# A vision block on one core: the mixer's two norms moved to ACT, the third Newton step to GpSimd

## What is computed

```python
# token mixer, per image: h is (256, 256)
y = sigmoid(q) * (ew @ (exp(k) * v)) / (ew @ exp(k))
h = y @ out_w + out_b + flatten(x)
h = (h - mean(h)) * rsqrt(var(h) + 1e-05) * ln_g + ln_b        # first norm

# a class token is put in front, then attention with mixed heads
xn = (h - mean(h)) / sqrt(var(h) + 1e-05)                      # second norm
q, k, v = split(xn @ w_qkv)                                    # 16 heads of 64
attn = softmax(q @ k.T / 8)
attn = einsum('bhij,hg->bgij', attn, reattn_w)                 # heads are mixed
attn = (attn - mean_g(attn)) * rsqrt(var_g(attn) + 1e-03)      # norm over the 16 heads
h = h + (attn * gamma + beta) @ v @ w_out + b_out

# feed-forward with quantized activations and ternary weights
h = h + quant(silu(quant(norm(h)) @ w_gate.T) * (... @ w_up.T)) @ w_down.T
```

## Time and profile before

| what | value |
|---|---|
| median of 3 runs | 852.46 us (850.26 to 853.55) |
| the profiled execution | 854.99 us, its span 853.2 us |
| busy: PE, DVE, ACT, POOL | 81%, 66%, 51%, 25% of the span |
| mean granted PE clock | 0.933 of full |

### The profile page before, as it was taken

The page is one execution under the profiler, slowest core; times in us unless marked ns, Lnnn a source line. Parts: engine busy times, 40 slices in busy tenths (PEclk is TensorE's granted clock), DMA queues, the critical chain, the costliest instruction groups (busy, mean ns, idle before and its releaser), DMA issues.

```text
span 853.2 us, 18885 instructions
## 1 busy us (share of the span) xinstructions
PE 691.6 (81%) x7618; PEld 483.0 (57%) x7634; DVE 566.3 (66%) x1215; ACT 436.1 (51%) x1231; POOL 212.2 (25%) x399
## 2 busy tenths in 40 slices
PE   0859758997889978998899888987899789757654
PEld 0546545766567646765576656764676567535421
DVE  0596647566876788568956786678767885559333
ACT  0103706583566657473748354755666574738311
POOL 0307224102430154014411233024301540033000
PEclk9959967999799999999999979999999999979977
DMA  8400560047102531145005610362025301450000
GB/s 317 159 1 6 176 240 2 1 147 250 40 3 77 187 141 33 45 157 203 33 15 173 216 32 2 112 232 93 2 79 198 129 8 50 152 202 10 1 12 1
DMA packets 42395, 83.98 MB, mean 98 GB/s; under 512 B 3003, under 2 KB 6596, under 8 KB 41668
## 3 DMA queue, kind: packets, MB, share of 16 engines
q1 hardware_dynamic: 41268, 79.29, 27.0%
q10 hardware_dynamic: 1040, 3.49, 1.0%
HBM read 46.98 MB, written 35.79 MB: 97 GB/s over the span
## 4 chain that ended last, share of the span: by engine, by line
PE 39%; DVE 21%; DMA 21%; ACT 10%; issue 6%; POOL 2%; SPq 1%; POOLq 0%; ACTq 0%; DVEq 0%
DMA pg<-turned 12%; DMA turned<-pst 8%; PE big L546 7%; PE small L546 7%; PE big L563 6%; PE small L707 4%; DVE var L1246 4%; DVE an L1290 3%; ACT pst L941 3%; PE small L692 2%; PE big L640 2%; PE small L662 2%; ACT ot L1029 2%; ACT sqb L961 2%; DMA tok_b<-in_tok_b 2%
## 5 line engine op out<-in xcount | busy, mean ns | idle before, releaser
L941 ACT ACTIVATE pst<-big,nb 128x256 f32<-128x256 f32 x256 | 117.9, 474 | 32.0 <-DVE nb L1214 32.0
L1211 DVE TENSOR_REDUCE mx<-big 128x4 f32<-128x1024 f32 x64 | 78.3, 1223 | 52.3 <-PE big L563 51.6
L640 PEld LDWEIGHTS big<-pst,pg 64*64 64x64 f32 x4096 | 72.8, 149 | 52.5 <-DVE an L1290 28.3
L640 PE MATMUL big<-pst,pg 64*64 64x64 f32 x4096 | 80.6, 236 | 21.9 <-DVE an L1290 12.2
L961 ACT ACTIVATE sqb<-big 128x1024 f32<-128x1024 f32 x64 | 65.2, 1020 | 35.7 <-PE big L640 33.8
L1246 DVE TENSOR_REDUCE var<-sqb 128x64 f32<-128x1024 f32 x64 | 77.4, 1211 | 7.5 <-ACT sqb L961 7.5
L1290 DVE TENSOR_TENSOR an<-big,rstd 128x1024 f32<-128x1024 f32 x64 | 78.4, 1224 | 2.2
L662 PE MATMUL small<-w_qkv,xnv 128*128 128x512 f32 x128 | 69.9, 672 | 8.5 <-DVE h L1383 5.7
L563 PE MATMUL big<-qk_t 64*128 64x256 f32 x512 | 72.6, 402 | 3.8 <-ACT qk_t L924 3.7
L692 PE MATMUL small<-an,v 128*64 128x130 f32 (+1 forms) x768 | 56.6, 289 | 21.2 <-ACT ot L1029 20.6
L546 PE MATMUL small<-xnt,w_qkv 128*128 128x256 f32 x256 | 63.8, 392 | 0.0
(11 more groups left out here) (201 smaller groups left out, 1262.8 us busy)
## 6 DMA issues: line engine op xcount, KB each, us to landing
turned<-pst SPq DMA_DIRECT2D x128, 257.0 KB
pg<-turned SPq DMA_DIRECT2D x16, 2056.0 KB, 11.0
w_qkv<-in_w_qkv SPq DMA_DIRECT2D x1, 3072.0 KB
xt<-in_x_t SPq DMA_DIRECT2D x8, 256.0 KB, 2.9
xr<-in_x_tok SPq DMA_DIRECT2D x8, 256.0 KB, 2.7
out<-h SPq DMA_DIRECT2D x16, 128.0 KB
an<-in_gate_t ACTq DMA_DIRECT2D x1, 1024.0 KB, 8.6
an<-in_up_t ACTq DMA_DIRECT2D x1, 1024.0 KB, 10.9
```

What stands on the lines that cost most here:

```text
L640: last = mm(mix_place(n)[half[0]:half[1], k_hi * 512 + i * 64:k_hi * 512 + (i + 1) * 64], pg[rows, ib, j], w_rows[rows, it, ib, :], start= ...
L941: last = A(pst[:, g % 2, h % GH, it * T:(it + 1) * T], big[p % 2][:, (j * TT + it) * T:(j * TT + it + 1) * T], ACT.Exp, bias=nb[:, h, it:i ...
L1211: V.reduce_max(mx[:, hs, :], big[p % 2][:, :].rearrange("p (h t l) -> p h t l", h=2, t=TT), AX)\
```

## The change

The two norms of the mixer are taken from DVE. POOL makes, after each power -0.5, an offset per row, `sh_a` = -mean times `rs_a`, in two operations (`shift`), and ACT applies scale and offset in one Identity per 128 rows (`mixer_norm` on ACT). The first norm stands on ACT between square(0) and root(0), the second between root(5) and values(1, 1). POOL's `tok_g` and PE's `mixer_turn` wait for ACT instead of DVE. In each of the 8 tiles, the third Newton step becomes two operations on POOL, a TENSOR_SCALAR that adds -3 and a product with y, and DVE's L1277 goes; DVE waits for the last of them.

```diff
+        sh_a = sb("sh_a", [P, TT])
...
-        pool_r = stage("pool_r", [x for n in mixes for x in [(y, n) for y in ("x", "yy", "w")]
+        pool_r = stage("pool_r", [x for n in mixes for x in [(y, n) for y in ("x", "yy", "w", "w3", "n3")]
...
@@ tensor: mixer_turn
-                    pe.wait_ge(dve_a.sem, dve_a.at(b, ("n2", tt)))
+                    pe.wait_ge(act_a.sem, act_a.at(b, ("n2", tt)))
@@ scalar
+            def mixer_norm(b, src, dst, rs, step):
+                act.wait_ge(pool_a.sem, pool_a.at(b, rs))
+                for tt in range(TT):
+                    A(dst[:, tt, :], src[:, tt, :], ACT.Identity, bias=sh_a[:, tt:tt + 1], scale=rs_a[:, tt:tt + 1])\
+                        .then_inc(act_a.sem, 1)
...
-            def begin_mixing(b):
+            def begin_mixing(b, first_norm):
                 square(b, 0)
+                if first_norm:
+                    mixer_norm(b + 1, h2, h2, "sh", "n")
                 root(b, 0)
...
                     elif n == 5:
+                        if do_scores:
+                            mixer_norm(b + 1, h2, xn, "sh2", "n2")
                         values(b, 1, 1)
...
+            mixer_norm(0, h2, h2, "sh", "n")
+            mixer_norm(0, h2, xn, "sh2", "n2")
             mixer_turned(0)
@@ vector
-            def mixer_first_norm(b):
-                norm_apply(b, dve_a, h2, h2, P, range(TT), mv_a, rs_a, pool_a, "rs")
-
...
-            def mixer_norm(b):
-                norm_apply(b, dve_a, h2, xn, P, range(TT), mv_a, rs_a, pool_a, "rs2")
...
-                    dve.wait_ge(pool_r.sem, pool_r.at(b, ("w", n)))
-                    V.scalar_tensor_tensor(out=rstd[:, n % 2, :], in0=nww[:, n % 2, :], scalar=-3.0, in1=y0[:, n % 2, :],
-                                           op0=ALU.add, op1=ALU.mult).then_inc(dve_r.sem, 1)
-                    dve.wait_ge(dve_r.sem, dve_r.at(b, ("n3", n)))
+                    dve.wait_ge(pool_r.sem, pool_r.at(b, ("n3", n)))
...
-                    elif n == 4 and do_scores:
-                        mixer_norm(b + 1)
...
-                ffn_h(b, ff, P, 1, None, (lambda: mixer_first_norm(b + 2)) if do_mixer else None,
+                ffn_h(b, ff, P, 1, None, None,
@@ gpsimd
+            def shift(b, step):
+                pool.wait_ge(pool_a.sem, pool_a.at(b, step))
+                G.tensor_tensor(sh_a[:], mv_a[:, :, 0], rs_a[:], ALU.mult).then_inc(pool_a.sem, 1)
+                pool.wait_ge(pool_a.sem, pool_a.at(b, step + "m"))
+                G.tensor_scalar(sh_a[:], sh_a[:], -1.0, 1.0, ALU.mult, ALU.mult).then_inc(pool_a.sem, 1)
...
             def mixer_out(b):
                 power(b, pool_a, dve_a, ve_a, rs_a, P, slice(0, TT), "ve")
-                pool.wait_ge(dve_a.sem, dve_a.at(b, ("n", 1)))
+                shift(b, "rs")
+                pool.wait_ge(act_a.sem, act_a.at(b, ("n", 1)))
...
             def mixer_norm(b):
                 power(b, pool_a, dve_a, ve_a, rs_a, P, slice(0, TT), "ve2")
+                shift(b, "rs2")
...
                 G.tensor_tensor(w, x, w, ALU.mult).then_inc(pool_r.sem, 1)
+                pool.wait_ge(pool_r.sem, pool_r.at(b, ("w", n)))
+                G.tensor_scalar(w, w, -3.0, 1.0, ALU.add, ALU.mult).then_inc(pool_r.sem, 1)
+                pool.wait_ge(pool_r.sem, pool_r.at(b, ("w3", n)))
+                G.tensor_tensor(rstd[:, n % 2, :], w, y, ALU.mult).then_inc(pool_r.sem, 1)
```

More of the change, by code:

```diff
@@ L293, in build @@
         pe_a = stage("pe_a", [("kv", 0), ("kv", 1), "q", "den", "num", "h", "xt"])
-        act_a = stage("act_a", [("ek", 0), ("ek", 1), "tanh", "xt"])
+        act_a = stage("act_a", [("ek", 0), ("ek", 1), "tanh", ("n", 0), ("n", 1), ("n2", 0), ("n2", 1), "xt"])
         dve_a = stage("dve_a", [("kv", 0), ("kv", 1), "rd", "t", "y", "h1", ("st", 0), ("st", 1), ("ag", 0),
-                                ("ag", 1), "ve", ("n", 0), ("n", 1), ("st2", 0), ("st2", 1), ("ag2", 0),
-                                ("ag2", 1), "ve2", ("n2", 0), ("n2", 1)])
-        pool_a = stage("pool_a", ["res", ("ekv", 0), ("ekv", 1), "rs", "g", "b", "rs2"])
+                                ("ag", 1), "ve", ("st2", 0), ("st2", 1), ("ag2", 0), ("ag2", 1), "ve2"])
+        pool_a = stage("pool_a", ["res", ("ekv", 0), ("ekv", 1), "rs", "rsm", "sh", "g", "b", "rs2", "rs2m", "sh2"])
         pool_h = stage("pool_h", ["hold"])
         pool_x = stage("pool_x", ["xnv"])
-        pool_r = stage("pool_r", [x for n in mixes for x in [(y, n) for y in ("x", "yy", "w")]
+        pool_r = stage("pool_r", [x for n in mixes for x in [(y, n) for y in ("x", "yy", "w", "w3", "n3")]
                                   + (["qx", "qyy", "qw", "cyy", "cw"] if n == 4 else [])])
@@ L326, in build @@
                 + {5: ["qn3", "cn3", "qa", "ca"]}.get(n, [])\
-                + [("n3", n), ("a", n)] + {0: [("v", 1)], 1: ["qv"]}.get(n, [])
+                + [("a", n)] + {0: [("v", 1)], 1: ["qv"]}.get(n, [])
         pe_r, act_r, dve_r = stage("pe_r", r_order), stage("act_r", sq_order), stage("dve_r", a_order)
@@ L1077, in iteration @@
                 if do_scores:
-                    begin_mixing(b + 1)
+                    begin_mixing(b + 1, do_mixer)
                 ffn_h(b, ff, P, 1)
@@ L1095, in _ @@
             mixer_tanh(1)
-            begin_mixing(0)
+            begin_mixing(0, True)
             iteration(0, True, True)
@@ L1450, in _ @@
             mixer_out(0)
-            mixer_first_norm(0)
             mixer_stats(0)
-            mixer_norm(0)
             then(V.reduce_sum(mix_mean, mix_rep, AX))
@@ L1517, in _ @@
             mixer_out(1)
-            mixer_first_norm(1)
             variance(0, 0)
```

## The result

The changed kernel takes a median of **865.0 us** (863.7 to 865.3, four runs) against 851.4 us (849.3 to 853.6, four runs) of the kernel before on the same chip: a ratio of 1.016 [1.013, 1.019], slower. The profiled execution took 865.25 us, with a span of 863.4 us, 10.2 more than before; the difference of the medians is 13.7, since the profiled execution of the kernel before was itself 3.6 us above its median.

The account below looks back on a forecast made before the run. The prediction took a chain of waits as the bound, its half up to L509 nearly all on DVE. 854.99 + 4.0 (waits) + 7.8 (clock falls) = 866.8, put at 864 us against the run median; range 843 to 873.

Parts of the forecast that it names:

- The start of the half: From L1242 to a(0): POOL already arrives last there, and a(0) would start 1.2 us late (1.0 to 1.3).
- The norm path: First norm going POOL, ACT, POOL instead of DVE: `tok_g` would start 0.6 us late.
- ACT is free there: At the first norm, ACT would start its two Identities without waiting; 1.0 us for both.
- The collision: DVE's L1374 meets POOL's `tok_b` under an exclusive lock, waits, takes over 1 us, and pushes POOL's last operations near 406.1.
- The tiles: Loop after a(0): lateness +1.4 us at a(1), +0.9 at a(3), +1.2 at a(4), and L509 0.5 us late.
- The sum of the waits: Later starts over the whole kernel: 3.0 us for six halves, 1.0 for images 0 and 7, setup 0; +4.0 us.
- The falls of the clock: PE idles longer before L640, so its clock falls in 4 of 6 halves, not 2, 3.9 us each: +7.8 us.
- Five Newton steps: Third Newton steps counted on DVE between a(0) and L509, 0.25 us each, 1.25 us in all.
- rival 1: a(0) keeps its time and halves shorten by 1.9 to 2.6 us: 837 to 841 us, partly 845; chance 0.2.
- DVE's relief passes through: Work taken off DVE shortens each half if a(0) keeps its time: 837 to 841 us, partly 845; chance 0.2.
- Waits without falls: The late starts cost 4.0 us but PE's clock falls no more often: 856.5 us; chance 0.2.
- POOL the bound of every tile: Slow POOL operations and handovers add 0.25 us per tile chain, and the clock falls in all six halves: 876 us; chance 0.08.

Follow-up runs that it names:

- run 3: The change without its Newton part, only the two norms moved to ACT: 855.0 us, ratio 1.003 against the kernel before.
- run 4: Only the third Newton step moved to POOL, both norms staying on DVE: 862.9 us, ratio 1.017 against the kernel before.
- run 6: The changed kernel with 4 and 7 unused products on PE in its waits for `hq` and a(0): 854.8 us, ratio 1.007 against the kernel before.
- run 5: The kernel before with four useless POOL operations in newton(0), only to delay a(0): 865.0 us, ratio 1.018.
- run 7: The kernel before with only the second norm moved to ACT, its two shift operations on POOL: 840.7 us, ratio 0.989.
- run 8: Run 7's kernel with the third Newton step on POOL for tiles 2 and 3 only: 841.5 us, ratio 0.988 against the kernel before.
- run 1: The kernel before with 4 and 6 unused products on PE in its waits for `hq` and a(0): 850.1 us, ratio 1.001.
- run 2: The changed kernel with 6 and 11 unused products on PE in the same two waits: 861.6 us, ratio 1.014 against the kernel before.
- run 9: The kernel before with 3 and 4 unused products on PE in the same two waits: 849.9 us, ratio 0.999.
- run 10: Run 7's kernel with 3 and 4 unused products on PE in the same two waits: 837.8 us, ratio 0.986 against the kernel before.

## Why the prediction was right, and where not

The forecast was 864 us, slower; it is 865.0. That is 13.7 us more than before by the medians, where 11.8 were forecast. The cause, a later a(0) and the clock behind it, is the one that was forecast; that the total is within 1 us is partly luck, as the fifth point shows. The steps held as follows.

- **The start of the half** held nearly to the number. `tok_g` was to begin at about 5.0 us, and does at 4.94. The norm path was put at +0.6 us and measured 0.67 in the timeline and 0.68 by itself (run 3); the two POOL operations at +0.5, and 0.48 and 0.47 (run 4). ACT's pair of Identities was put at 1.0 us and takes 1.09. a(0) is 1.15 us late in four halves (forecast 1.2), and 1.5 and 1.8 in the other two. There "ACT is free there" did not hold: the norm had to wait its turn in ACT's list, which PE held up while its clock was low (the rows of ACT in the last section).
- **The collision** is there: r1 takes 1.59 us, "over 1 us" as forecast. But it does not carry the delay. `tok_g`'s lateness of 0.67 us reaches the end of x y y as 0.67. From `tok_g` to a(0) it is 5.20 us where r1 waits for `tok_b` (10.14 - 4.94), and 5.17 and 5.06 where `tok_b` waits for r1 (10.50 - 5.33, 10.80 - 5.74), so which of the two goes first hardly matters for a(0). What no collision at all would save was not tried.
- **The tiles.** Where the clock is full (run 6), a(1) is +1.45 us (forecast +1.4), a(2) +1.20, a(3) +0.94 (+0.9), a(4) +1.35 (+1.2), and L509 +0.67 (+0.5): 26.85 us, forecast 26.7. POOL is last before a(0), a(1) and a(4), as said.
- **The sum of the waits** was +4.0 us: 3.0 for six halves, 1.0 for images 0 and 7, 0 for the setup. Six halves at 0.67 are 4.0. The other term was mis-sized in both directions: setup and image 0's half gained 1.7 us, the tail lost 1.5, as far as one execution of each kernel can tell.
- **The falls of the clock** were the weakest step, "4 of 6, 3.9 us each, +7.8 us". It is six of six, but each is cheaper: the halves stand 1.2 to 4.0 us above 26.85, 14.9 us in all (1.0 of them the later `tok_g` of two halves), against 6 x (27.48 - 26.18) = 7.8 before, so +7.1 us. The sum came out near because number and size missed to opposite sides. The estimate behind it, that more idle time of the same kind makes falls likelier, is borne out by run 5; the price of a fall, taken from the earlier trace rows alone, was not. The two falls of before came from an execution with a mean clock of 0.933, at the low end of that kernel's executions (0.930 to 0.953), so that two in six may be too many for it; no further profile settles this.
- **A slip.** Five Newton steps (n = 1 to 5) were counted ahead of L509. The PE row above shows L509 released by `ack` (L1269), which DVE makes ahead of a(5). The earlier trace rows name L1277 for the kernel before, but there too `mixer_turn` waits for `ca`, the step of `ack`, and L509 starts 0.14 us behind `ack`'s end (421.56 + 0.41 to 422.11), just when L1277 happens to end; so only four Newton steps stood on that path, 1.0 us and not 1.25. The forecast didn't use the sum, but rival 1's prices did.

The rivals. *DVE's relief passes through* falls for the change as it was made, since a(0) didn't keep its time. Its condition was the right one: run 7 keeps a(0), and the relief passes through in full, 0.69 us a half. *Waits without falls* (856.5 us) falls with the six halves; run 6 takes most falls away and gives 854.8. *POOL the bound of every tile* (876 us) wanted 0.4 us for a TENSOR_SCALAR on POOL and 0.1 for a handover; the rows have 0.24 us and 0.09 (592.25 + 0.32 to 592.66). The Trainium skill, "GPSIMD Engine Reference", section "Engine selection", speaks against moving elementwise work to GpSimd. The trace agrees as far as it goes: L1603 and L1605 with their handovers take 0.77 us from the end of x y y to a(0), where L1277 took 0.29. These are two operations in the place of one, and no operation of this kind was run on both engines.

What stays open is what decides between a fall and none in a given half. The runs show only that behind PE's longer waits for `hq` and a(0) it fell in six of six (after, runs 3 and 5) and three of six (run 4), behind the shorter ones in two or one of six (before and run 8, run 7), and behind waits with products in them in none (runs 1, 2, 6, 9 and 10). With products there the profiled executions have falls in other places, four and five instead of two in the kernel before; whether the products bring these about is not shown.

## What to carry to other kernels

Before work is taken from the busiest engine, find the places where the engine that receives it already arrives last: here one microsecond there cost more than all that was freed. Move the piece that does not stand ahead of such a place, and only that: the second norm alone turns 1.6% slower into 1.1% faster. And price a new wait of PE at what its clock loses behind it, too.

## What was not expected of the hardware

- A delay of 1.1 us of one tile per image cost 15.0 us (run 5). In the profile, PE's wait for a(0) grew from 1.08 to 2.18 us, and of the 10.7 us that six halves lost, at least 4.1 are the granted clock.
- The collision of DVE and POOL goes either way within one kernel. In the half from 305.89 r1 was first by a hair, and took 0.75 us; POOL's `tok_b` was slow, and r2 then waited for it in its turn, 1.64 us instead of 0.69:

```profile
312.40 0.75 DVE L1375 TENSOR_SCALAR sqb<-sqb,s2u 128x1024 f32<-128x1024 f32 x1
313.19 1.64 DVE L1379 TENSOR_SCALAR hq<-sqb 128x1024 bf16<-128x1024 f32 x1
```
```profile
311.22 1.27 POOL L1572 TENSOR_TENSOR h<-h,tok_g 128x512 f32<-128x512 f32 x1 [1.60 <-ACT h L916]
312.57 1.71 POOL L1575 TENSOR_TENSOR h<-h,tok_b 128x512 f32<-128x512 f32 x1
```

The Trainium skill, "SBUF - State Buffer", section "SBUF: two separate sides", has the lock go to whichever instruction starts first, for its whole length. The rows agree: r1 still ran for 0.58 us when `tok_b` started, and `tok_b` took 1.71 us, 0.45 more than its usual 1.26. This is not why a(0) came at 10.50 us there instead of 10.15. `tok_g` was already 0.39 us late, because ACT was late: it had waited for PE's L736 until 306.44, and then 0.29 us for the L640 ahead of square(0), so that the norm started right behind square(0) at 310.06, and not when `sh_a` was ready at 309.62. In the half from 583.20 square(0) had ended by 586.08, ahead of `sh_a`:

```profile
309.14 1.02 ACT L967 ACTIVATE sqb<-big 128x1024 f32<-128x1024 f32 x1 [0.29 <-PE big L640]
310.06 1.08 ACT L916 ACTIVATE h<-h,sh_a,rs_a 128x256 f32<-128x256 f32 x2
```

- A TENSOR_SCALAR on POOL (L1603, 128 x 64) takes 0.24 us, less than the product of two tensors of that size, 0.32.
